# Macaron layer on one core: first expert block's shared tile last, first batch loaded and normalised beside it, row of maxima in halves, splits redistributed

## What is computed

```python
x = x + 0.5 * ffn(layernorm(x))
x = x + attn(layernorm(x))
x = x + 0.5 * ffn(layernorm(x))

def ffn(x):      # 8 experts, 256 -> 512 -> 256, one per token
    route = sigmoid(x @ router_w)
    e, p = argmax(route), max(route)
    return p * ((silu(x @ gate_w[e]) * (x @ up_w[e])) @ down_w[e])

def attn(x):     # 16 query heads, 4 key/value heads, width 16, causal
    q, k, v = x @ Wq + bq, x @ Wk + bk, x @ Wv + bv
    return softmax(causal(q @ k.T / 4)) @ v
```

## Time and profile before

| | us |
|---|---|
| median of 3 runs (lowest to highest) | 416.62 (414.96 to 417.93) |
| profiled execution | 416.29 |
| its span | 414.5 |
| mean granted clock of TensorE, share of full | 0.978 |
| first expert block's last epilogue ends | 125.3 |
| first scores | 170.7 |
| second expert block's last epilogue ends | 403.5 |

### The profile page before, as it was taken

The page is one execution under the profiler, slowest core; times in us unless marked ns, Lnnn a source line. Parts: engine busy times, 40 slices in busy tenths (PEclk is TensorE's granted clock), DMA queues, the critical chain, the costliest instruction groups (busy, mean ns, idle before and its releaser), DMA issues.

```text
span 414.5 us, 8450 instructions
## 1 busy us (share of the span) xinstructions
PE 374.9 (90%) x3164; PEld 294.5 (71%) x3171; DVE 243.0 (59%) x732; ACT 143.7 (35%) x296; POOL 175.3 (42%) x288
## 2 busy tenths in 40 slices
PE   8999999999998698888999999998699999999980
PEld 6769999999673455555566665555399999989660
DVE  5889852222222647778878778889757874222220
ACT  3221111111110234565767657577334111111110
POOL 1041425552111254556767664565812215643111
PEclk9999999999999979999999999999989999999996
DMA  8959932299103524202213042200211101398000
GB/s 266 409 207 351 333 106 76 66 334 333 40 16 114 156 81 126 56 20 78 78 48 105 20 121 71 55 28 28 59 57 37 43 25 56 103 345 318 27 23 14
DMA packets 27055, 50.04 MB, mean 121 GB/s; under 512 B 4458, under 2 KB 20590, under 8 KB 25975
## 3 DMA queue, kind: packets, MB, share of 16 engines
q1 hardware_dynamic: 19118, 25.10, 18.7%
q0 software_dynamic: 4512, 21.50, 15.1%
q10 hardware_dynamic: 3376, 2.80, 2.3%
HBM read 35.16 MB, written 6.55 MB: 101 GB/s over the span
## 4 chain that ended last, share of the span: by engine, by line
PE 67%; DVE 17%; DMA 5%; issue 4%; SPq 3%; ACT 1%; another core or an unknown queue 1%; POOL 1%; POOLq 0%; DVEq 0%; ACTq 0%
PE bank L1003 25%; PE bank L1024 13%; PE bank L1228 3%; PE bank L1457 3%; PE bank L1485 3%; PE bank L1386 2%; PE bank L542 2%; DVE mxa L1416 2%; PE bank L993 2%; PE bank L965 2%; PE bank L1514 2%; SPq L1333 1%; PE bank L1379 1%; DVE area L1534 1%; PE bank L592 1%
## 5 line engine op out<-in xcount | busy, mean ns | idle before, releaser
L1003 PEld LDWEIGHTS bank<-area,W 128*128 128x128 f32 x1024 | 119.9, 193 | 3.5 <-ACT area L1093 1.7
L1003 PE MATMUL bank<-area,W 128*128 128x128 f32 x1024 | 120.9, 277 | 1.2 <-ACT area L1093 1.2
L1172 DVE TENSOR_TENSOR area<-area,bank 128x512 f32<-128x512 f32 x34 | 23.4, 687 | 71.5 <-issue 49.7
L1464 ACT ACTIVATE area<-bank 128x512 f32<-128x512 f32 x96 | 54.2, 597 | 27.8 <-PE bank L1457 27.4
L1024 PE MATMUL bank<-W,area 128*128 128x256 f32 x256 | 60.9, 381 | 1.8 <-DVE area L1157 1.8
L1473 POOL TENSOR_SCALAR_AFFINE_SELECT area<-area 128x512 f32<-128x512 f32 x64 | 40.8, 650 | 40.5 <-ACT area L1464 40.2
L1104 ACT ACTIVATE area<-bank 128x512 f32<-128x512 f32 x34 | 20.3, 597 | 97.1 <-PE bank L1003 87.5
L1024 PEld LDWEIGHTS bank<-W,area 128*128 128x128 f32 x256 | 46.2, 190 | 7.9 <-issue 2.9
L1416 DVE TENSOR_REDUCE mxa<-bank 128x2 f32<-128x512 f32 x64 | 42.9, 673 | 7.2 <-PE bank L1388 7.1
L892 POOL DMA_INDIRECT out<-area,sidx x17 | 17.1, 1005 | 55.3 <-DVE area L1157 52.6
L892 POOL DMA_INDIRECT x2d<-area,sidx x17 | 17.1, 1006 | 54.7 <-DVE area L1157 54.7
(11 more groups left out here) (200 smaller groups left out, 574.3 us busy)
## 6 DMA issues: line engine op xcount, KB each, us to landing
W<-wall SPq DMA_DIRECT2D x24, 512.0 KB, 8.8
area<-area SPq DMA_DIRECT2D x48, 128.0 KB, 2.4
area<-x SPq DMA_DIRECT2D x8, 256.0 KB, 5.3
area<-x2d SPq DMA_DIRECT2D x8, 256.0 KB, 4.6
rows<-area ACTq DMA_DIRECT2D x8, 256.0 KB, 2.5
area<-JV SPq DMA_DIRECT2D x40, 32.0 KB, 1.9
cb<-constb ACTq DMA_DIRECT2D x1, 296.0 KB, 4.4
area<-x,gidx POOLq DMA_INDIRECT x18, 3.5
```

The source lines that it names most:

```text
L1003: last = pe.matmul(ps[:, i * P:(i + 1) * P], W[:, w:w + P], xT[:, j % 2, c, :], start=(c == 0), stop=(c == C - 1))
L1172: v.tensor_tensor(out, sil[:, n % 2, :], bank[2 + n % 2][:], ALU.mult).then_inc(f_h[l], 1)
L1464: a.activation(PT[:, n % 2, u * 512:(u + 1) * 512], bank[u][:], ACT.Exp, scale=D ** -0.5).then_inc(a_e, 1)
```

## The change

`MIX` becomes one number per block: in the first block the shared tile goes last (place 16), in the second it stays at 15. `shared_gate_up` holds its gate and up products in pieces, and in the first block the down products of the tile before stand between the pieces. The first batch of `x2d` is loaded when the last up product is done and scatters 0 to 15 have landed; batches 1 to 7 still wait for `fin`. Its statistics, Newton steps and normalisation (`first_norm`) stand in `ffn_dve` behind the last epilogue. In the second block the last down product goes to bank 7.

LN_GROUPS becomes batch 0; 1; 2 to 4. The shift before the first guess of 1/sqrt is gone: one multiplication by -0.5 does both. The second batch's subtractions go from GpSimd to VectorE. The first batch's row of maxima goes out in halves (`a_neg_dve`, `a_neg_pe`, `a_neg_copy`, `a_max_row` now count rows e, of which 0 and 1 are the halves of batch 0). Only four groups of maxima stand ahead of the loop; iterations 0, 1 and 2 take two groups each, from then on n + 7 as before. Fillers: 12 and 20 instead of 48, 8, 3 and the 12 single ones.

```diff
-MIX = 15
+MIX = (2 * NE, 2 * NE - 1)
-WARM_MID = 48
+WARM_MID = 12
+WARM_NEXT = 20
...
-        LN_GROUPS = (((0, BA), (BA, B)), ((0, 1), (1, 4), (4, 5)))
+        LN_GROUPS = (((0, BA), (BA, B)), ((0, 1), (1, 2), (2, BA)))
...
-            link(nc.vector.tensor_scalar(hv[:, t0:t1], ve[:, t0:t1].bitcast(I32), 1, None,
-                                         ALU.arith_shift_right), seen)
-            nc.vector.tensor_scalar(rs[:, t0:t1], hv[:, t0:t1], -1.0, RSQRT_MAGIC,
+            nc.vector.tensor_scalar(rs[:, t0:t1], ve[:, t0:t1].bitcast(I32), -0.5, RSQRT_MAGIC,
                                     ALU.mult, ALU.add).then_inc(s_st[k], 1)
...
+        def down_bank(l, n):
+
+            return bank[7] if l == 1 and n == NP - 1 else bank[6]
...
-            if n >= 1:
+            if n >= 1 and down_bank(l, n) is bank[6]:
                 pe.wait_ge(f_o[l], n)
...
+                if j != MIX[l]:
+                    ffn_gate_up(l, j, offs[j])
+                else:
+                    shared_gate_up(l, 0, (0,))
+                    if j == NP - 1:
+                        ffn_down(l, j - 1, offs[j - 1])
+                    shared_gate_up(l, 0, (1,))
+                    shared_gate_up(l, 1, (0, 1))
...
             finish(NP - 1)
+            if l == 0:
+                first_norm(seen)
             further(NP, tiles_over(v, l))
...
+        def maxima(n):
+
+
+            return (NG + 2 * n, NG + 2 * n + 1) if n < 3 else (n + NG + 3,)
...
+            h0, h1 = ((0, NH // 2), (NH // 2, NH))[e] if e < 2 else (0, NH)
+            sp.wait_ge(a_ms, e + 1)
+            sp.dma_start(Qs[MROWS:MROWS + 1, r, h0:h1].rearrange("o h s -> o (h s)"), mT[h0:h1]).then_inc(a_mq[r], 16)
...
-            sp.wait_ge(s_fin[0], 1)
+            sp.wait_ge(f_up[0], NP)
+            for i in range(OB):
+                sp.wait_ge(f_s[0][i], 16 * (2 * NE // OB))
             for b in range(B):
+                if b == 1:
+                    sp.wait_ge(s_fin[0], 1)
...
             ln_newton(1, 1, seen)
+            ln_newton(1, 2, seen)
             ln_apply(2, p)
             ln_apply(3, p)
-            a_split_dve2(1, p)
-            a_split_dve3(1, p)
             a_split_dve2(2, p)
+            a_mask(0)
             a_split_dve3(2, p)
-            ln_newton(1, 2, seen)
-            a_mask(0)
...
             ln_transpose(1, 0, PRO_T[0])
             a_proj_q(0, PRO_Q[0])
             a_proj_kv(0, PRO_KV[0])
+            warm(WARM_NEXT)
             ln_transpose(1, 1, PRO_T[1])
             a_vt_pe(0, PRO_KV[0])
-            warm(8)
             a_proj_q(1, PRO_Q[1])
             a_proj_kv(1, PRO_KV[1])
-            a_vt_pe(1, PRO_KV[1])
-            warm(3)
-            for m in range(NG + 3):
...
+            for m in range(NG):
...
                 for x in own[1:]:
+                    a_max_pe(x, 1)
+                    a_max_pe(x, 2)
```

More of the change, by code:

```diff
@@ L178, in macaron @@
         ve = sb("ve", [P, NT])
-        hv = sb("hv", [P, NT], I32)
         rs = sb("rs", [P, NT], I32)
@@ L1053, in ffn_pe @@
             pe = nc.tensor
-            offs = [(tile_of(j) % NE) * WE for j in range(NP)]
+            offs = [(tile_of(l, j) % NE) * WE for j in range(NP)]
             for j in range(NP):
@@ L1707, in _ @@
             ffn_dve(0, seen)
-            for t in range(*tiles(1, 0)):
-                ln_sums(1, t, seen)
-            ln_stats(1, 0, seen)
-            ln_newton(1, 0, seen, v)
-            ln_apply(0)
             for t in range(*tiles(1, 1)):
@@ L1851, in _ @@
-                if m == NG - 1:
-                    pe.wait_ge(s_xs[1], 4)
-                    a_neg_pe(0)
-                if m == NG + 1:
-                    pe.wait_ge(s_one, 32)
-                    for u in range(3):
-                        a_scores(0, u)
+            pe.wait_ge(s_one, 32)
+            pe.wait_ge(a_v, 2)
+            for u in range(3):
+                a_scores(0, u)
+            a_neg_pe(1)
             for n in range(NG * B):
                 b, g = divmod(n, NG)
-                m = n + NG + 3
+                own = maxima(n)
+                m, more = own[0], m_left(n)
```

335 lines of the change are left out of this document (197 added, 138 removed).

## The result

| | before | after |
|---|---|---|
| median, us | 417.95 | 415.08 |
| ratio, 95% interval | | 0.9926 [0.9904, 0.9949] |
| profiled execution / its span | 416.29 / 414.5 | 413.18 / 411.4 |

(before: 20 runs in turn with the changed kernel.) The change gains 3.1 us by the ratio. The forecast was 7.8, and 415.08 lies above the range's end of 413.8. Direction right, size wrong.

What follows compares the result with a forecast made beforehand. A chain of latencies with filler matmuls between 125 and 171 was taken to bound what the change could win. Terms: -13.7 to the first values product, +5.7, -0.6, -0.2, +1.0 = -7.8, 408.5 (408.8 beside the median); range 404.8 to 413.8.

Steps and rivals of the forecast that it cites:

- The step that failed: Before the first maxima: stack DMAs split over two queues land by 142.9, first maximum's product at 143.5, 10.7 earlier.
- The second batch: Between expert block and attention: load lands at 133.6, Newton steps take 3.3, transposes start at 139.3, 5.0 earlier.
- I expect no fall of the clock here: Ahead of the second batch's transposes: twenty fillers (4.3 us) fill the formerly idle hole, so projections run at full rate.
- the fillers were needed: Rival, between 143.5 and 158: with fewer fillers the clock falls and comes back, +4, giving 412.8; chance 0.14.
- What is late next: After the first batch comes 6.6 earlier, the second batch, not the first, is the next one late.
- the third batch's norm: Before the first scores: due at 149.3, ready at 148.4; contention could make it 0.8 later, just in the way.
- signs of being wrong: Clock falling between 143 and 175, maxima row or stack landing late, or VectorE idle over 6 before iterations 0-2 reductions.
- they are on VectorE's path, so I charge all of it: The second batch's four subtractions, moved from GpSimd, cost VectorE 2.2 between the reductions, charged in full.
- The catch-up: Three maxima groups inside iterations 0 to 2 give back 5.7; iteration 4's values product comes 8.0 earlier.
- catch-up nearly free: Rival: idle time in both engines absorbs the maxima moved into iterations 0 to 2; 1.4 instead of 5.7, 404.5; chance 0.12.
- The catch-up and the queue take all: Rival: maxima moved into the iterations cost 8 instead of 5.7, batch 3's stack late by 1.5; 412.6; chance 0.13.
- The first batch's transposes: Behind the first expert block: an earlier load brings them from 137.01 to 130.45, 6.6 earlier.

Runs made afterwards that it cites:

- e1_loads: The changed kernel with batches 5 to 7 and the constant rows loaded behind the first two batches' stack DMAs; 412.31 us, 0.9946 of before.
- e6_late_loads: The changed kernel with constant rows loaded behind the first batch's stack, batches 5 to 7 behind the half row of maxima; 412.56 us, 0.9864 of before.
- e8_loads_vt: e6_late_loads with ScalarE's copy of the second batch's V put ahead of its stack DMAs; 412.24 us, 0.9876 of before.
- the control: The changed kernel itself, run again without an edit; 414.85 us, 0.9927 of before.
- e3_hold: The changed kernel with 16 fillers put in front of the first maxima; 412.45 us, 0.9929 of before.
- e14_norm_split: e13_norm_hold with second batch's subtractions on GpSimd, ScalarE's third-batch copy ahead of the waiting casts, half row sent earlier; 411.02 us, 0.9805 of before.
- e16_fill_28: e14_norm_split with 28 instead of 34 fillers ahead of the second batch's transposes; 409.76 us, 0.9828 of before.
- e13_norm_hold: e9_norm with 34 instead of 20 fillers ahead of the second batch's transposes; 413.76 us, 0.9875 of before.
- e9_norm: e8_loads_vt with the third batch's statistics beside the second's and its Newton steps right behind them; 411.87 us, 0.9861 of before.

## Why the prediction was wrong

**The step that failed** is "The twelve stack DMAs of the first batch are split between the queues of SyncE and ScalarE and land by 142.9. So the first maximum's product … comes at 143.5". They landed at 148.9. Two terms were left out. SyncE needs some 0.6 to issue each of its eight, one behind another, so the last is issued by 142.67: with the 2.4 of before's landings, 145.1. And they share the DMA engines with seven loads that SyncE issued just ahead, so a landing takes 6.1 to 6.2: another 3.8. The rows for both were in the trace: SyncE's queue was read only at 183 to 193, and the DMA share of these microseconds not at all. The change starts the stack 4.5 us earlier (137.80, before 142.27), and the prediction did not ask what would be on the queues at that time; before, the 16 engines had been idle from 139 to 141. Restoring the landings (e1_loads, e6_late_loads, e8_loads_vt) moved the first maxima by 3.3 to 5.3.

**The second batch** was 2.2 late as well, hidden under the stack: with the stack in time the first maxima would have come at 145.65, when its projections ended, and not at 143.5. Its load was seen landed at 134.97, not 133.6 (0.65 of this is the later start of the execution), and GpSimd's twelve Newton steps took 4.1, not 3.3: some were longer while VectorE subtracted (up to 0.67 instead of 0.20). That is the contention which the prediction read from the earlier trace rows and charged to the third batch only.

**"I expect no fall of the clock here"** held in this execution from 135 to 147, and not in the control, where it was down from 144 (0.66 to 147). In the changed kernel it fell behind the hole that was left, from 149 to 156, and in other variants behind other holes. The rival "the fillers were needed" gave 4 for it. Measured on the way to the scores it cost half a microsecond, no more than two profiles of one kernel differ by, where it was back before the third batch's projections (the changed kernel against e3_hold), 1.2 in e14_norm_split against e16_fill_28, and 2.2 where it fell on them (e13_norm_hold against e9_norm). And fillers are not free: in eight of the sixteen profiled executions that have them, the twelve after the expert block ran at 1.2 GHz, 3.9 to 4.5 us instead of 2.5 to 2.8, and held back rows that were ready. The others mostly paid for it with the hole ahead of the second batch. The first profile did the one and the control the other, with equal times (413.18 and 413.25).

**What is late next** was named only in part. The second batch it was, but behind the stack. Had only the DMA been in the way, e8_loads_vt would have had its scores 13.1 behind its first maxima, at 158.5; they came at 160.54. There the third batch's norm stood in the way: due at 149.3 and forecast for 148.4, it was done at 150.5 in the changed kernel and at 151.4 in e8_loads_vt. Behind that come VectorE's subtractions, and with all of them the clock. Each undone alone gave, by the ratio, from nothing (e1_loads, e3_hold) to 2.6 us (e6_late_loads), all together 4 to 5. That is about the 4.7 between forecast and measurement, though those kernels are no longer the predicted one.

Two of the prediction's own signs of being wrong came: the clock fell between 143 and 175, and a stack landed after TensorE had asked for it.

**Right, in part by luck:** the stretch from the first maxima to iteration 4: 40.2 forecast, 40.8 measured. Within it errors cancel. The scores took 13.1 (13.7 forecast): "they are on VectorE's path, so I charge all of it" has the right mechanism, but of the 2.2 charged 1.2 showed, and the fall of the clock that is in the 13.1 was not in the forecast. The catch-up, from the values product of iteration 0 to that of iteration 4, went from 17.26 to 24.12: **5.7 was mis-sized, it measured 6.9**, near the bound of 8. Little of VectorE's idle time in the earlier trace rows could be used, and the rival "catch-up nearly free" is ruled out. "The catch-up and the queue take all" came closest to the time, 412.6, for the wrong reason: the second row was issued at 182.30, not 176.8, and no scores waited for it.

**Right:** the tail of the second block gave 0.65 (0.6, and 0.2 for the rounds). The end of the first block is 1.1 later net of the start, 0.9 forecast. The first batch's transposes were 4.0 earlier, not 6.6, of which about 2 is the slow fillers: its rows were ready at 130.93.

## What to carry to other kernels

When a step is moved earlier, look at the DMA queues and the DMA share at its new time: the issue time of every DMA ahead on the same queue, and the bytes still under way, count as much as the engine's work. A stretch that is a chain of latencies over five engines has its limits one close behind another, so removing the first gives only the distance to the second; add up the next two or three before promising the whole, and test them together, since each alone can look worthless. For filler matmuls, work out when they end at either clock: ending late they hold back rows that are ready, ending early they leave a hole behind which the clock falls. Before one edit is credited with the difference of two profiles, compare their granted clocks too.

## What was not expected of the hardware

Stack DMAs of 128 KB took 2.4 us from issue to landing with no loads ahead of them and 6.1 behind 1.8 MB of loads on the same engines, and the small ones of 32 KB on ScalarE's queue as long (6.1, before 2.5): another queue did not bring them past. In the control both took longer still, 7.5 and 7.3.

The same kernel at the same place ran the same twelve fillers in 2.76 in one execution and at 1.2 GHz (4.20 for 11) in another, after an idle gap of 2.44 in both. The granted clock behind that gap is thus not a fixed property of the kernel. For twelve fillers the two outcomes lie up to 1.7 us apart (2.76 and 4.45).
